# A mixture-of-experts block: expert tokens turned by way of DRAM and VectorE, slot weights turned by way of DRAM

## The reference

```python
x = x + 0.5 * ffn(layernorm(x)); x = x + attn(layernorm(x)); x = x + 0.5 * ffn(layernorm(x))

def ffn(x):                                  # 8 experts, the top 2 of each token
    probs = softmax(x @ gate_w + gate_b, over the tokens)
    vals, idx = top_k(probs, 2)
    h = relu(x @ w1[e] + b1[e]); h = relu(h @ w2[e] + b2[e]); y = relu(h @ w3[e] + b3[e])
    v[e] = sum over the tokens that chose e of y * their weight for e
    return for each token: the sum of v[e] over its two experts
```

## Time and profile before

| | |
|---|---|
| Median of 3 runs | 2112.66 us (2111.5 to 2114.31) |
| Profiled execution | 2125.24 us, of which the span 2123.5 |
| PE busy | 2046.4 us (96%) |
| DVE busy | 1820.4 us (86%) |
| ACT busy | 1600.1 us (75%) |
| POOL busy | 416.1 us (20%) |
| Packets of the DMA queues | 70394, 94.36 MB |

### The profile page before, as it was taken

One profiled execution on the slowest core, in us unless ns is written; L12 is line 12 of the kernel. 1 busy time (PEld: TensorE's weight loads), 2 busy tenths in 40 slices (PEclk: granted clock), 3 DMA queues, 4 the chain that ended last, 5 costly groups with the idle time before them and its releaser, 6 DMA issues.

```text
span 2123.5 us, 99873 instructions
## 1 busy us (share of the span) xinstructions
PE 2046.4 (96%) x43655; PEld 1587.4 (75%) x43659; DVE 1820.4 (86%) x4031; ACT 1600.1 (75%) x3315; POOL 416.1 (20%) x1118
## 2 busy tenths in 40 slices
PE   5899989999999999999999999999999999979998
PEld 3788866377778777777777777777777776758885
DVE  6666666899999999999999999999999994766665
ACT  5244446599999999999999999999999998424442
POOL 1333303411121111111111111111121111023330
PEclk8799989999999999999999999999999999979998
DMA  8211103400010000100001001000010001231112
GB/s 273 73 47 45 47 16 117 142 30 24 14 33 12 27 28 10 34 17 21 31 7 34 22 17 33 9 30 24 14 34 13 26 5 51 72 118 49 42 50 87
DMA packets 70394, 94.36 MB, mean 44 GB/s; under 512 B 16640, under 2 KB 59396, under 8 KB 69956
## 3 DMA queue, kind: packets, MB, share of 16 engines
q1 hardware_dynamic: 62796, 68.75, 10.1%
q0 software_dynamic: 6816, 19.20, 3.4%
q10 hardware_dynamic: 344, 0.01, 0.0%
HBM read 62.24 MB, written 25.43 MB: 41 GB/s over the span
## 4 chain that ended last, share of the span: by engine, by line
PE 89%; DVE 5%; issue 2%; ACT 1%; POOL 1%; SPq 1%; DMA 0%; another core or an unknown queue 0%; ACTq 0%; DVEq 0%; POOLq 0%
PE bank L1257 39%; PE bank L1250 22%; PE bank L1132 17%; PE bank L1339 3%; PE bank L1143 1%; PE bank L1367 1%; PE bank L1300 1%; PE bank L1150 1%; DVE stats L1397 1%; PE bank L1021 1%; SPq L698 0%; POOL work L591 0%; DVE work L1586 0%; PE bank L1210 0%; PE bank L1307 0%
## 5 line engine op out<-in xcount | busy, mean ns | idle before, releaser
L964 ACT ACTIVATE feat<-bank 128x512 f32<-128x512 f32 (+3 forms) x2304 | 1263.4, 565 | 112.9 <-PE bank L1257 12.6
L1257 PE MATMUL bank<-work 96*32 96x512 bf16 (+2 forms) x15872 | 1207.0, 370 | 5.1 <-DVE work L1764 3.8
L1764 DVE TENSOR_REDUCE work<-bank 128x1 f32<-128x512 f32 (+1 forms) x1920 | 1179.9, 661 | 25.7 <-PE bank L1257 22.9
L1250 PE MATMUL bank<-feat,phase 128*17 128x128 f32 (+3 forms) x18432 | 881.4, 263 | 0.3 <-ACT feat L970 0.3
L1250 PEld LDWEIGHTS bank<-feat,phase 128*17 128x17 f32 x18432 | 592.4, 98 | 267.0 <-ACT feat L970 13.8
L1257 PEld LDWEIGHTS bank<-work 96*32 96x32 bf16 (+1 forms) x15872 | 475.0, 96 | 56.7 <-DVE work L1764 24.3
L1132 PE MATMUL bank<-work 128*128 128x256 f32 (+1 forms) x1872 | 399.1, 364 | 4.2 <-issue 2.9
L1132 PEld LDWEIGHTS bank<-work 128*128 128x128 f32 x1872 | 325.5, 192 | 41.0 <-issue 4.4
L625 POOL TENSOR_SCALAR_AFFINE_SELECT feat<-feat 128x128 f32<-128x128 f32 x512 | 146.1, 295 | 455.0 <-ACT feat L964 438.6
L1648 DVE COPY work<-phase 128x514 f32 x234 | 101.6, 436 | 124.8 <-ACT work L878 101.0
L578 POOL DMA_INDIRECT work<-token_table,row_no x142 | 138.1, 973 | 302.7 <-PE bank L1143 145.5
(11 more groups left out here) (201 smaller groups left out, 1379.2 us busy)
## 6 DMA issues: line engine op xcount, KB each, us to landing
phase<-in_w SPq DMA_DIRECT2D x12, 1024.0 KB, 12.0
work<-qk_parts SPq DMA_DIRECT2D x60, 192.0 KB
token_table<-rows SPq DMA_DIRECT2D x8, 1056.0 KB, 8.7
work<-work SPq DMA_DIRECT2D x512, 0.5 KB
qk_parts<-phase SPq DMA_DIRECT2D x20, 384.0 KB, 2.7
work<-qk_parts SPq DMA_DIRECT2D x60, 128.0 KB
qk_parts<-work SPq DMA_DIRECT2D x12, 384.0 KB, 2.6
x_res<-in_x SPq DMA_DIRECT2D x8, 512.0 KB
```

The costliest lines, as they stand in the source:

```text
L964: eng.activation(p_ring[:, n % P_RING, lo:QB], s_bank("probs", n)[:, lo:QB], ACT.Exp, scale=HD ** -0.5).then_inc(sig.s_done, 1)
L1250: mm = eng.matmul(bank[ACC_BANK][GRID * g:GRID * g + VW, GRID * i0:P], v_aug[:, t, h, :], weights[:, i0:TPJ, g, :], start=(t == 0), stop=( ...
L1257: mm = eng.matmul(out[GRID * g:GRID * (g + 1), width], left[:, GRID * g:GRID * (g + 1)], right, start=start, stop=stop)
L1764: eng.tensor_reduce(maxima[:, h % 2, j, PLACE[i], at:at + 1], scores[:, 0:hi - lo], AX_X, ALU.max).then_inc(sig.a_done, 1)
```

## The change

In both phases, for all tiles from the fifth on (`DIRECT` = 4), PE and ACT no longer turn the tokens. SP stores each half of `x_slot` to DRAM (`tile_rows`) and loads the tile again in four DMAs of 32 partitions each, so that the 32x32 blocks stand where they belong in the turned tile but are not turned themselves; they land in `to_turn`, a ring of two tiles in `rows`. DVE then turns all blocks of the tile with one 32x32-block transpose (`turn_tile`), straight into `acts[:, 0]`. The gather waits for the store instead of for PE's transposes. For all tiles the weights take another way: DVE no longer widens them, ACT stores them to DRAM (`slot_weights`) as they are, one per partition, and loads them in the next step as a row, broadcast to all partitions. PE's weight transposes and ACT's copies of them are gone. The first layer's input now has the order half, feature block, slot.

```diff
+DIRECT, TURN_RING = 4, 2
...
+        slots_dram = [nc.dram_tensor(f"tile_rows{f}", (N_SUB, KD, P, P), F32).ap() for f in range(2)]
+        weights_dram = [nc.dram_tensor(f"slot_weights{f}", (N_SUB * P,), F32).ap() for f in range(2)]
...
+        acts_in = acts[:, 0].rearrange("p b k s -> p b (k s)")
...
-        w_wide = carve(2 * TS * P).rearrange("p (b u s) -> p b u s", b=2, u=TS)
...
+        to_turn = rows[:, :, :].rearrange("p i r -> p (i r)")[:, 0:TURN_RING * TS * D].rearrange(
+            "p (b s) -> p b s", b=TURN_RING)
...
-                need.wait_ge(sig.xt[f], KD * subs_before(j - NXG + 1))
-                need.wait_ge(sig.w_col[f], 3 * (j - NXG + 1))
+                if j - NXG < DIRECT:
+                    need.wait_ge(sig.xt[f], KD * subs_before(j - NXG + 1))
+                else:
+                    need.wait_ge(sig.slot_stored[j % NXG], 16 * stored_uses(f, j - NXG))
+                need.wait_ge(sig.w_col[f], 2 * (j - NXG + 1))
...
+            def store_slots(f, j):
+                for u, n in enumerate(SUBS[j]):
+                    need.wait_ge(sig.slot[j % NXG][u], 16 * slot_uses(f, j, u))
+                    eng.dma_start(slots_dram[f][n].rearrange("k p f -> p k f"),
+                                  x_slot[:, j % NXG, u, 0:D].rearrange("p (k f) -> p k f", k=KD),
+                                  ).then_inc(sig.slot_stored[j % NXG], 16)
+
+            def load_to_turn(f, j):
+                n = len(SUBS[j])
+                tile = slots_dram[f][SUBS[j][0]:SUBS[j][0] + n]
+                need.wait_ge(sig.slot_stored[j % NXG], 16 * stored_uses(f, j))
+                need.wait_ge(sig.table[f], 16 * GROUPS)
+                need.wait_ge(sig.tile_turned[f], j - TURN_RING - DIRECT + 1)
+                for a in range(P // GRID):
+                    eng.dma_start(to_turn[GRID * a:GRID * (a + 1), j % TURN_RING, 0:n * D].rearrange(
+                        "p (u f) -> p u f", f=GRID),
+                        tile[:, :, :, GRID * a:GRID * (a + 1)].rearrange("u k (b r) f -> r (u k b) f", r=GRID),
+                        ).then_inc(sig.turn_loaded[j % TURN_RING], 16)
+
+            def tiles(f):
+                for j in range(DIRECT, N_TILES):
+                    store_slots(f, j)
+                    if j > DIRECT:
+                        load_to_turn(f, j - 1)
+                load_to_turn(f, LAST)
...
+            tiles(0)
...
+            tiles(1)
...
-                need.wait_ge(sig.xt[f], KD * subs_before(j + 1))
-                need.wait_ge(sig.layer[f][0], j - 1)
-                eng.activation(acts[:, 0, j % 2, :, 0:WIDTH[j]],
-                               bank[0][:, :].rearrange("p (k s) -> p k s", k=KD)[:, :, 0:WIDTH[j]],
-                               ACT.Copy).then_inc(sig.xt_copy[f], 1)
-                need.wait_ge(sig.w_tr[f], subs_before(j + 1))
+                if j < DIRECT:
+                    need.wait_ge(sig.xt[f], KD * subs_before(j + 1))
+                    need.wait_ge(sig.layer[f][0], j - 1)
+                    eng.activation(acts_in[:, j % 2, 0:KD * WIDTH[j]], bank[0][:, 0:KD * WIDTH[j]],
+                                   ACT.Copy).then_inc(sig.xt_copy[f], 1)
+
+            def store_weight(f, j):
+                if j >= N_TILES:
+                    return
+                need.wait_ge(sig.w_col[f], 2 * (j + 1))
+                eng.dma_start(weights_dram[f][SUBS[j][0] * P:SUBS[j][0] * P + WIDTH[j]].rearrange("(u p) -> p u", p=P),
+                              w_col[:, j % 2, 0:len(SUBS[j])], allow_slow_non_contiguous=True,
+                              ).then_inc(sig.w_stored[j % 2], 16)
+
+            def load_weight(f, j):
+                if not 0 <= j < N_TILES:
+                    return
+                need.wait_ge(sig.w_stored[j % 2], 16 * (f * len(range(j % 2, N_TILES, 2)) + j // 2 + 1))
                 need.wait_ge(sig.weighted[f], KD * (j - W_RING + 1))
-                eng.activation(w_row[:, j % W_RING, 0:WIDTH[j]], bank[1][:, 0:WIDTH[j]],
-                               ACT.Copy).then_inc(sig.w_row[f], 1)
+                need.wait_ge(sig.w_loaded[j % 2], 16 * (f * len(range(j % 2, N_TILES, 2)) + j // 2))
+                eng.dma_start(w_row[:, j % W_RING, 0:WIDTH[j]],
+                              weights_dram[f][SUBS[j][0] * P:SUBS[j][0] * P + WIDTH[j]].unsqueeze(0).to_broadcast(
+                                  [P, WIDTH[j]])).then_inc(sig.w_loaded[j % 2], 16)
...
+                    load_weight(f, n - 1)
+                    store_weight(f, n)
...
-                    need.wait_ge(sig.xt_copy[f], j + 1)
+                    need.wait_ge(sig.xt_copy[f], min(j + 1, DIRECT))
+                    need.wait_ge(sig.tile_turned[f], j - DIRECT + 1)
...
+                        if l == 0:
+                            act = acts_in[:, b, 0:KD * WIDTH[j]].rearrange("p (u k s) -> p k u s", k=KD, s=P)[:, k]
+                        else:
+                            act = acts[:, l, b, k, 0:WIDTH[j]]
...
             def transpose_tile(f, j):
+                if j >= DIRECT:
+                    return
...
-            def transpose_weight(f, j):
-                need.wait_ge(sig.w_col[f], 3 * (j + 1))
-                need.wait_ge(sig.w_row[f], j)
-                for u in range(len(SUBS[j])):
-                    eng.transpose(bank[1][:, u * P:(u + 1) * P], w_wide[:, j % 2, u],
-                                  ident[:, :]).then_inc(sig.w_tr[f], 1)
...
-                        transpose_weight(f, j)
...
-                    transpose_weight(f, j)
...
+                need.wait_ge(sig.w_stored[b], 16 * (f * len(range(b, N_TILES, 2)) + j // 2))
                 eng.tensor_reduce(w_col[:, b, 0:n], w_pick[:, b, 0:n], AX_X, ALU.add).then_inc(sig.w_col[f], 1)
-                need.wait_ge(sig.w_col[f], 3 * j + 2)
-                need.wait_ge(sig.w_tr[f], subs_before(j - 1))
-                eng.tensor_copy(w_wide[:, b, 0:n], bc(w_col[:, b, 0:n], 2, [P, n, P])).then_inc(sig.w_col[f], 1)
...
+            def turn_tile(f, j):
+                need.wait_ge(sig.turn_loaded[j % TURN_RING], 16 * (P // GRID) * turn_uses(f, j))
+                need.wait_ge(sig.layer[f][0], j - 1)
+                eng.transpose(acts_in[:, j % 2, 0:KD * WIDTH[j]],
+                              to_turn[:, j % TURN_RING, 0:KD * WIDTH[j]]).then_inc(sig.tile_turned[f], 1)
...
-                need.wait_ge(sig.w_row[f], j + 1)
+                need.wait_ge(sig.w_loaded[j % 2], 16 * (f * len(range(j % 2, N_TILES, 2)) + j // 2 + 1))
...
+                    if j - 1 == LAST:
+                        turn_tile(f, LAST)
                     if 0 <= j - 3 < N_TILES:
                         weigh(f, j - 3)
+                    if DIRECT <= j - 1 < LAST:
+                        turn_tile(f, j - 1)
                     stage(f, j - 1, 2)
                     if 0 <= j - 2 < LAST:
```

More of the change, by code:

```diff
@@ L256, in slot_uses, with stored_uses, turn_uses @@
     return f * len(fills) + sum(n <= j for n in fills)
+def stored_uses(f, j):
+    fills = [n for n in range(DIRECT, N_TILES) if n % NXG == j % NXG]
+    return f * sum(len(SUBS[n]) for n in fills) + sum(len(SUBS[n]) for n in fills if n <= j)
+def turn_uses(f, j):
+    fills = [n for n in range(DIRECT, N_TILES) if n % TURN_RING == j % TURN_RING]
+    return f * len(fills) + sum(n <= j for n in fills)
 class Waits:
@@ L301, in __init__ @@
         self.staged, self.xt, self.xt_copy = many("staged", 2), many("tile_tr", 2), many("tile_copied", 2)
-        self.w_col, self.w_tr, self.w_row = many("weight_col", 2), many("weight_tr", 2), many("weight_row", 2)
+        self.slot_stored, self.turn_loaded = many("slot_stored", NXG), many("turn_loaded", TURN_RING)
+        self.tile_turned = many("tile_turned", 2)
+        self.w_col, self.w_stored = many("weight_col", 2), many("weight_stored", 2)
+        self.w_loaded = many("weight_loaded", 2)
         self.layer = [many(f"layer_mm{f}_", LAYERS) for f in range(2)]
@@ L1008, in transpose_rows @@
                         if n == 1:
-                            need.wait_ge(sig.xt_copy[0], N_TILES)
-                            need.wait_ge(sig.w_row[0], N_TILES)
+                            need.wait_ge(sig.xt_copy[0], DIRECT)
                         if n == 2:
@@ L1131, in layer @@
                     for k in range(KD):
+                        if l == 0:
+                            act = acts_in[:, b, 0:KD * WIDTH[j]].rearrange("p (u k s) -> p k u s", k=KD, s=P)[:, k]
+                        else:
+                            act = acts[:, l, b, k, 0:WIDTH[j]]
                         mm = eng.matmul(bank[bk][:, m * TILE:m * TILE + WIDTH[j]],
-                                        staged[:, b, l, k * D + m * P:k * D + (m + 1) * P], acts[:, l, b, k, 0:WIDTH[j]],
+                                        staged[:, b, l, k * D + m * P:k * D + (m + 1) * P], act,
                                         start=(k == 0), stop=(k == KD - 1))
@@ L1142, in transpose_tile @@
                     for k in range(KD):
```

(18 more changed lines are left out.)

## The result

The changed kernel takes 2499.72 us (median of 4 runs, 2498.36 to 2504.49) against 2112.64 us: 1.1836 times as long, 95% interval 1.1821 to 1.1851. I had forecast 2092, with 2074 to 2118 as the range.

What follows compares the result with a forecast made beforehand. PE bounds the kernel; without its transposes a loop through DVE sets wide steps at 5.27 us instead of 5.84, narrow tiles lose 1.05. The 22.0 us gain from 2112.66, plus 1.3 for waits, gives 2092 us, range 2074 to 2118.

Steps and rivals of the forecast that it cites:

- the part on the feed: DMA path of tokens and slot weights: SP issues 3.2 us a step, engines 3.5, all covered by the 5.27 us step.
- I take 3: Landing of a token load or store in the feed: 3 us, from 384 KB stores that took 2.7.
- Rival 4: DMA engines become the bound at the load of 2048 short runs: slower, 2160 us or some 230 more; chance 0.18.
- 3.5 us a step: DMA engine time for a wide tile's 160 token runs per engine, taken between 2.4 and 8.7 us; covered.
- where the prediction lets the loss begin: Token runs on the DMA engines: slower than before from 30 ns a run on.
- The rule of the Trainium skill on rearranged patterns: Token load: a plain DMA transpose with a rearranged pattern is 19 times slower, 14 us a step; spoke against the change.
- The transpose of 128x512: DVE's 32x32-block transpose of a wide tile's tokens: 0.70 us, between bounds 0.30 and 1.21.
- DVE's loop: Layer 0, relu, staging copy, slot weight work, weighing, token transpose, layer 0: 5.27 us a wide step, against 5.84 before.
- the second loop: Layer 2 on PE, then weighing and token transpose on DVE, back to PE: 5.20 us a wide step.
- PE's own step: The layers' matmuls of a wide tile on PE once the transposes are gone: 5.18 us.
- the narrow tile costs 4.10: Step of a narrow tile, whose loop holds the next wide tile's transpose: 4.20 us against 3.15 before, 1.05 lost.
- The sum made of it, 22 us: Gain over both phases from 29 wide and 6 narrow tiles each plus early weight transposes: 22.0 us.

Runs made afterwards that it cites:

- e4: Changed kernel, but the slot weight store writes 512 B per slot instead of 4 B, slot weights left out of the result: 2103.83 us, against 2112.43 before the change.
- e1: Changed kernel with only the slot weights by way of DRAM; all tokens turned by PE and copied by ACT as before: 2467.79 us, ratio 1.1686.
- e6: As e1, but 64 B of the identity matrix stored per slot, side by side; slot weights left out: 2110.23 us, against 2120.84 before the change.
- e11: As e1, but each 4 B slot weight stored 64 B from the next; slot weights left out: 2097.47 us, against 2113.07 before the change.
- e5: As e1, but each 4 B slot weight stored 512 B from the next; slot weights left out: 2106.84 us, against 2120.84 before the change.
- e2: Changed kernel with only the tokens by way of DRAM and DVE; slot weights widened, turned and copied as before: 2112.02 us, ratio 1.0001.
- e8: Changed kernel, but DVE turns the slot weights so they are stored in 128 B runs, and does their work behind the second relu: 2112.01 us, ratio 0.9953.
- e12: e9 with DVE's slot weight work back at the head of the step, in front of the token transpose: 2092.14 us, ratio 0.9859.
- e9: e8 with DVE's transpose of the tokens moved in front of the weighing, for all tiles: ratio 0.9932.
- e10: e2 with DVE's slot weight work behind the second relu and the token transpose in front of the weighing: ratio 0.9924.
- e3: Changed kernel with four slot weight stores in flight instead of two, each load issued two steps after its store instead of one: 2764.28 us, ratio 1.3097.

## Why the prediction was wrong, point by point

**The step that failed** is one sentence of the part on the feed: "The slot weights are stored and loaded a step apart and needed two steps later." I priced that path at nothing; the only landing that I priced, "I take 3", was that of the tokens, on the row of the 384 KB stores. Two things were wrong in it.

First, a step apart isn't cover when it is closed. ACT's queue holds load n-1 and store n in that order, and the load waits for the landing of store n-1. I had asked when the weights are needed and not what is queued behind the wait. The period is landing + 0.33 + 0.04 and 0.02 of issue. With a landing of 3 us the loop is 3.4 us and would be harmless, as it is with the 3.7 of e4; the form of the code alone costs nothing.

Second, the landing. All my rows of stores had runs of 1024 B or more, and 1 KB in 256 runs of 4 B, side by side, isn't of that kind: 9.9 us, and 9.5 with the token traffic gone (e1). I gave bounds for the run of 128 B and none for the run of 4 B. The Trainium skill, "DMA: Bandwidth & Descriptors", section "Specifications", puts 512 B as the least transfer for line rate, since below it the engine reads, modifies and writes. The runs agree only in part: 64 B runs (e6) and single 4 B runs 64 or 512 B apart (e11, e5) are under 512 B too, and nothing waited for them. A read-modify-write of one piece of memory by neighbouring runs in turn would fit all four, but that mechanism is inferred; the runs show only the two conditions. It would also have to fit that the 256 runs of a wide tile take 9.5 us and the 128 of a narrow one 9.0 (e1): twice the runs hardly took longer.

**Rival 4 is wrong too**; that it gave the right sign is luck. It had the token load as the one place. By itself the token path costs 15 ns a run (e2). I had taken 3.5 us a step, 22 ns a run, between two bounds, and the lower one, 15 ns, was misread: 2.87 us was the time of an issue on SP's queue, and that bias load landed 10.3 to 10.9 us after its issue. That e2 measures the same 15 is chance. In the changed kernel itself a run took (0.213 x 2497.1 - 0.101 x 2123.5) x 16 / 170368 = 30 ns, just where the prediction lets the loss begin; but e2 moves the same runs at 15, so that price comes with the slow store. The DMA share of 0.84 is that of e4 too, which is faster than before. The rule of the Trainium skill on rearranged patterns ("DMA: Bandwidth & Descriptors", section "Rules for kernel authors"), which would have put 14 us on a step, isn't what these runs show: the whole token path fits in a 5.4 us step.

**What held.** The transpose of 128x512 takes 0.70 us, as read off two smaller shapes. The wide step by DVE's loop, forecast at 5.27, is 5.37 in e4. In e8 it is 5.37 by the second loop, forecast at 5.20: its two handovers, 0.26 together in my sum, take 3.87 - 3.46 = 0.41. PE's own step is 5.18. From the weighing of one narrow tile to that of the next, five wide tiles and a narrow one take 30.95 us in e8 (113.12 to 144.07), where the forecast has 5 x 5.27 + 4.20 = 30.55: the narrow tile costs 4.10, as read. The sum made of it, 22 us, is still more than what e8 gave (0.9953, 10 us of 2120.84). With e8's own steps it is 2 x (29 x 0.47 - 6 x 0.95) + 1.6 = 17.5, so 7 to 8 us remain that I haven't assigned. e4's single run gave 9.

**What the change can give** once its store is mended: e12, 1.4% or 30 us of the 43.8 that PE can lose. Against the changed kernel e12 has two edits: the turned row of slot weights, and the transpose of the tokens ahead of the weighing. The way there took three steps, and each uncovered the next: e8 removes the slow store and shows the loop by layer 2, e9 breaks that and shows the feed by the gather, e12 takes the move of the slot weight work back and so releases the gather sooner. e10 shows that the route of the slot weights isn't needed for half of that gain: with them on PE, 16 us.

## What to carry to other kernels

A wait for a DMA's landing on an in-order queue, with the next DMA of the same stream behind it, makes the landing the least period of the pipeline; look at what stands behind the wait before costing it at nothing. Price a landing by a row with runs of its own size and spacing, not by its bytes: a 1 KB store in neighbouring 4 B pieces took 9.9 us to land in the changed kernel, longer than the 9.0 of a store of 1056 KB, and one 0.21 us transpose, which makes 128 B runs of them, mended it. Before a DMA is issued with less lead, or in front of another, see what loop it closes (e3). A high DMA share says little: it stood at 0.84 in the changed kernel and in e4, which is faster than the kernel before.

## What the runs showed of the hardware

- A store of 128 or 256 runs of 4 B that lie side by side in DRAM lands after 9.0 to 9.9 us (medians of e1 and the changed kernel; the first of a phase after 6.6 and 7.3). With 4 B at a distance of 64 B it is 2.8 us (e11), with 512 B a run 3.7 us (e4); with 64 B a run side by side, or 4 B at 512 B, nothing waited for it (e6, e5).
- Such a store delays DMAs that are in flight beside it, of other queues too. A load issued right behind it landed after 8.2 us instead of 3.8 (e3, changed kernel). SP's 128 KB stores took 9.2 us to land in the changed kernel and 2.0 in e2; they also took 2.0 in e3, where they go out between the landing of one slow store and the issue of the next. POOL's gathers landed after 8.5 us in e1 and 2.8 in e11, which move the same number of packets and bytes.
- 128 B and 512 B runs between DRAM and SBUF cost 15 ns of packet time each on average (e2), and 30 ns beside the slow store (changed kernel).
- VectorE's 32x32-block transpose of float32 is linear in its columns: 302 ns at 128, 0.43 to 0.44 us at 256, 0.70 us at 512 (changed kernel, e4).
